# An LSTM scan whose wait for x's columns stands elsewhere, and a last attention written out by hand

## The chip, the cores and the metric

The kernel runs on one core of a Trainium2 chip. The metric is the device time of one execution in microseconds (us), the median over runs; lower is better. PE is TensorE, PEld its weight loads, DVE is VectorE, ACT is ScalarE, POOL is GpSimd and SP is SyncE, which here only issues DMAs.

## What is computed

Six layers run over 4 sequences of 512 tokens with 256 features: a gated recurrence, an LSTM with attention inside each step, a mixture of 8 experts, a second recurrence (here called the scan), a cross attention, and a mixture of 4 experts plus a shared one. Behind each stands a residual add and a layer norm without scale. Cut to the layers that the change touches:

```python
def step(carry, x_t):                       # the LSTM layer, 512 steps
    h, c, attn = carry
    gates = concat([x_t, attn]) @ W_ih.T + b_ih + h @ W_hh.T + b_hh
    i, f, g, o = split(gates, 4)
    c = sigmoid(f) * c + sigmoid(i) * tanh(g)
    h = sigmoid(o) * tanh(c)
    alpha = softmax((h @ Wq.T) @ context.T)  # over 512 source positions
    attn = tanh(concat([alpha @ context, h]) @ Wout.T + b_out)
...
x = layernorm(x + second_recurrence(x))
x = layernorm(x + softmax(q(x) @ k(ctx).T / 16) @ v(ctx))   # cross attention
x = layernorm(x + mixture(x))
```

## The kernel before, in words

Every engine has its own instruction list, and the lists meet at semaphores. A wait that is not yet met holds everything behind it on its engine.

**The LSTM.** Each step is one turn of a hardware loop (`Fori`) on PE, ACT, DVE, POOL and SP. The state has 256 hidden values in two halves, k = 0 and 1, so most names come in pairs: `c0`, `c1` for the cell, `h0`, `h1` for the hidden value. A turn of PE's loop (L938) begins with the attention scores: `part_scores(0, 0)` multiplies the first half of the hidden state with the keys (it waits for `h_ready[0]`), `part_scores(0, 1)` the second half (it waits for `h_ready[1]`). Then come softmax, the weighted sum, `select`, and `gates(t + 1)`. This last one starts with `o_gate_x_hid`, which adds x's share of the output gate. x's share of all gates was computed ahead of the scan and lies in DRAM (`xg_rows`). SP loads it step by step into the tile `lstm_xg` in two pieces: 12 KB for the three gates i, f, g and 4 KB for the output gate o. There is only one buffer, so SP issues the load of o's piece for the next step once PE has used the present one (`o_x_used`, in `gates`), and it signals `o_x_loaded`. Every wait of a loop compares a semaphore with a register, which the engine's sequencer computes from the turn's number.

On DVE a turn does: the transposes of the gates, `cell_products` and `new_cell` of half 0, the transpose of the output gate, `cell_products` of half 1, `new_hidden` of half 0, `new_cell` of half 1, `new_hidden` of half 1. `new_hidden` needs tanh of the cell from ACT, which needs `new_cell`.

**Behind the scan.** The second recurrence runs in slots (16 tiles of 32 steps and the output of the last tile). Beside it, as generators that give out work slot by slot, run the mixtures, the attention and their norms, in blocks (quarters) of 512 tokens. When the scan ends, the last matmuls of the third quarter's mixture and its norm are done, then the last quarter alone: the norm after the scan, the cross attention for the four batch entries, a norm, and the mixture of 28 chunks of weights. A norm (`StripNorm`) is a chain over three engines: mean (PE), deviation (DVE), squares (ACT), variance (PE), root (ACT), inverse (DVE), spread (PE), result (DVE).

## Time and profile before

| | |
|---|---|
| median of 3 runs | 5704.32 us (5700.22 to 5705.46) |
| the profiled execution: its own time | 5699.97 us |
| the profiled execution: its span | 5698.2 us |
| PE busy in the span | 91% |
| VectorE busy | 59% |
| ScalarE busy | 34% |
| the LSTM's scan, from about 191 us to 3903 us | 3712 us, 65% of the span |
| from 5460 us to the start of the last mixture's chunks at 5526.5 us | 66.5 us |

The span runs from the first to the last instruction of the trace; the execution's own time is 1.8 us longer. All times of rows below count from the span's start. PE's busy share alone doesn't tell a bound, since matmuls overlap each other; the idle time in front of a group, and who ended it, says more.

### The profile page before, as it was taken

To read this page: it belongs to the slowest core of one execution; us is meant where nothing else is said; L and a number is where in the kernel's file an instruction comes from. 1 tells how busy PE (TensorE), PEld (TensorE's weight loads), DVE (VectorE), ACT (ScalarE), POOL (GpSimd) and SP (SyncE) were. 2 spreads that over 40 slices of the span, in tenths; PEclk is the share of its full clock that TensorE was granted. 3 is DMA by queue.
4 is the path that set the end of the run, shared out by engine and by line. 5 is a ranking of instruction groups with operands and counts; after the bars stand their busy time and mean duration, and the time that the engine had idled before them with its cause. 6 is when DMAs were issued, how large, how long until landed. Compare 5 with 4: busy or idle time off the path is not lost. (4 is left out here: it accounts for less than half of the span.)

```text
span 5698.2 us, 474379 instructions
## 1 busy us (share of the span) xinstructions
PE 5170.7 (91%) x214184; PEld 4093.5 (72%) x214184; DVE 3385.5 (59%) x15403; ACT 1942.1 (34%) x7968; POOL 340.9 (6%) x795
## 2 busy tenths in 40 slices
PE   9899999999999999999999999998688879796989
PEld 4788888888888888888888888887434334443433
DVE  5455555555555555555555555554798999999941
ACT  2244444344444443444444434442212222222221
POOL 0000000000000000000000000000111111111100
PEclk9999999999999999999999999999899889897999
DMA  2000000000000000000000000002111101010111
GB/s 97 38 2 2 2 2 2 2 2 2 2 2 2 2 2 2 2 2 2 2 2 2 2 2 2 2 2 76 56 52 39 41 17 56 26 58 23 51 39 57
DMA packets 60806, 111.58 MB, mean 20 GB/s; under 512 B 18308, under 2 KB 28452, under 8 KB 60204
## 3 DMA queue, kind: packets, MB, share of 16 engines
q1 hardware_dynamic: 59276, 109.42, 6.3%
q10 hardware_dynamic: 1440, 1.06, 0.1%
q8 instruction: 46, 0.75, 0.1%
q14 instruction: 44, 0.36, 0.0%
HBM read 99.92 MB, written 10.52 MB: 19 GB/s over the span
## 5 line engine op out<-in xcount | busy, mean ns | idle before, releaser
L868 PE MATMUL lstm_part_ps<-lstm_keys,lstm_hid 128*8 128x64 f32 x65536 | 1041.8, 219 | 200.2 <-DVE lstm_hid L1039 200.2
L868 PEld LDWEIGHTS lstm_part_ps<-lstm_keys,lstm_hid 128*8 128x8 f32 x65536 | 920.1, 90 | 342.3 <-DVE lstm_hid L1039 313.5
L891 PE MATMUL lstm_ctx_ps<-lstm_values,lstm_alpha 128*8 128x128 f32 (+1 forms) x49152 | 1029.1, 237 | 0.0
L891 PEld LDWEIGHTS lstm_ctx_ps<-lstm_values,lstm_alpha 128*8 128x8 f32 x49152 | 919.1, 90 | 23.5
L1061 DVE TENSOR_REDUCE lstm_neg_max<-lstm_part_ps 128x1 f32<-128x64 f32 x1024 | 230.0, 225 | 729.0 <-PE lstm_part_ps L868 729.0
L1021 DVE STREAM_TRANSPOSE lstm_gates<-lstm_half_ps 128x96 f32<-128x96 f32 x1026 | 290.2, 283 | 588.6 <-PE lstm_half_ps L826 564.3
L826 PE MATMUL lstm_half_ps<-lstm_w_hid,lstm_hid 128*25 128x96 f32 x16384 | 578.9, 248 | 1.2 <-issue 1.2
L1000 ACT ACTIVATE lstm_expo<-lstm_part_ps,lstm_neg_max 128x64 f32<-128x64 f32 x1024 | 320.8, 313 | 621.1 <-DVE lstm_neg_max L1061 621.1
L826 PE MATMUL lstm_half_ps<-lstm_w_attn,lstm_attn 128*25 128x96 f32 x16448 | 437.0, 246 | 0.0
L989 ACT ACTIVATE lstm_cell<-lstm_gates 128x12 f32<-128x12 f32 x1024 | 225.3, 220 | 431.1 <-DVE lstm_gates L1021 431.1
L2115 ACT ACTIVATE mix_gated<-mix_gate_ps 128x512 f32<-128x512 f32 (+1 forms) x192 | 107.8, 561 | 743.3 <-PE mix_gate_ps L1842 738.4
L1852 PE MATMUL mix_up_ps<-mix_xw,mix_ring 128*128 128x512 f32 (+1 forms) x704 | 313.0, 580 | 41.0 <-DVE mix_weighted L2419 31.0
L826 PEld LDWEIGHTS lstm_half_ps<-lstm_w_attn,lstm_attn 128*25 128x25 f32 x16448 | 350.0, 104 | 0.2 <-issue 0.2
L1872 PE MATMUL mix_down_ps<-mix_weighted,mix_ring 128*128 128x512 f32 (+2 forms) x768 | 346.8, 575 | 0.8 <-DVE mix_weighted L2419 0.7
L1842 PE MATMUL mix_gate_ps<-xT,mix_ring 128*128 128x512 f32 (+2 forms) x768 | 346.6, 575 | 0.0
L826 PEld LDWEIGHTS lstm_half_ps<-lstm_w_hid,lstm_hid 128*25 128x25 f32 x16384 | 345.0, 104 | 1.4 <-issue 1.4
L1099 POOL TENSOR_TENSOR xT<-xT,lstm_attn 128x8 f32 x512 | 104.9, 205 | 3620.5 <-ACT lstm_attn L1014 3620.5
L826 PE MATMUL lstm_half_ps<-lstm_xg,lstm_masks 128*25 128x96 f32 x8224 | 311.9, 254 | 9.0 <-DVE lstm_attn L1047 9.0
L2392 DVE TENSOR_TENSOR rw_terms<-rw_state,rw_sc 128x384 f32<-128x384 f32 x512 | 296.7, 580 | 6.7
L997 ACT ACTIVATE lstm_tanh_c<-lstm_cell 128x4 f32<-128x4 f32 x1024 | 210.4, 205 | 194.6 <-DVE lstm_cell L1032 155.0
L1039 DVE SCALAR_TENSOR_TENSOR lstm_hid<-lstm_o_col,lstm_tanh_c 128x4 f32<-128x4 f32 x1024 | 171.1, 167 | 173.5 <-ACT lstm_tanh_c L997 139.2
L1872 PEld LDWEIGHTS mix_down_ps<-mix_weighted,mix_ring 128*128 128x128 f32 (+1 forms) x768 | 143.0, 193 | 182.3 <-issue 163.4
(333 smaller groups left out, 8485.7 us busy)
## 6 DMA issues: line engine op xcount, KB each, us to landing
mix_ring<-in_sm_chunks SPq DMA_DIRECT2D x112, 384.0 KB, 3.1
mix_ring<-in_mix_chunks SPq DMA_DIRECT2D x80, 384.0 KB, 3.1
lstm_xg<-xg_rows SPq DMA_DIRECT2D x514, 12.0 KB
lstm_xg<-xg_rows SPq DMA_DIRECT2D x513, 4.0 KB
xg_rows<-rec_lam SPq DMA_DIRECT2D x16, 512.0 KB, 2.6
xT<-in_xT SPq DMA_DIRECT2D x4, 512.0 KB, 9.3
ctxT<-in_ctxT SPq DMA_DIRECT2D x1, 2048.0 KB, 14.5
out_xT<-xT SPq DMA_DIRECT2D x4, 512.0 KB, 3.9
```

What stands on the lines that cost most here:

```text
L826: mm = pe.matmul(ps[j * STRIP:j * STRIP + ROWS, :], rows, w[:, j * HID + cols.start:j * HID + cols.stop], start=start, stop=stop)
L868: mm = pe.matmul(part_rows(score_ps[part], b), hid[:, k, lo:lo + SPACE], keys[:, k, b * SRC + c * SUB:b * SRC + (c + 1) * SUB], start=(n = ...
L891: mm = pe.matmul(part_rows(ctx_ps[n], b), alpha[:, b, c, SPACE - 1 - 2 * c:2 * SPACE - 1 - 2 * c], values[:, b * SC + c, ctx_cols[n]], sta ...
L989: act.activation(cell[:, k, 0:GATES - 1, :], by_batch(turned), ACT.Tanh).then_inc(half_tanh[k], 1)
L997: act.activation(tanh_c[:, k, :], cell[:, k, GATES - 1, :], ACT.Tanh, scale=0.5).then_inc(c_tanh[k], 1)
L1000: act.activation(expo[:, part, :], score_ps[part], ACT.Exp, bias=neg_max[:, part:part + 1]).then_inc(exp_ready, 1)
L1021: dve.transpose(gates[:, k, :], half_ps[k]).then_inc(half_turned[k], 1)
L1061: dve.tensor_reduce(neg_max[:, part:part + 1], score_ps[part], AX_X, ALU.max, negate=True)\
L1842: mm = pe.matmul(gate_ps[0:m, 0:width], ring[:, at, k * P:k * P + m], token_block(x, i)[:, k, :], start=(k == 0), stop=(k == KC - 1))
L1852: mm = pe.matmul(up_ps[lo:lo + piece, 0:width], ring[:, at, col:col + piece], xw[:, x.buffer(e), k, 0:width] if e < x.x.routed else token_ ...
L1872: mm = pe.matmul(down_ps[:, o_, 0:width], ring[0:m, gn % RING, lo + o_ * P:lo + (o_ + 1) * P], gw[0:m, gn % 2, 0:width], start=(n == 0), s ...
L2392: dve.tensor_tensor(terms[:, :, :, :], before.unsqueeze(1).to_broadcast([P, 3, HALF, HD]), sc[:, parity, UNIT_KEY:RECV + 1, t, :].unsqueez ...
```

## The change

Three edits. First, PE no longer waits for `o_x_loaded` inside `gates`: the wait stands at the top of the loop's turn, ahead of the scores, with the same threshold (the piece that `gates(t + 1)` of this turn will use). Second, on VectorE `new_cell` of half 1 comes ahead of `new_hidden` of half 0. Third, the last quarter's attention is a function of its own: its norm uses buffers and PSUM banks that the scan has left, it is interleaved with the third quarter's norm, and the four batch entries' scores have a bank each.

```diff
                 def o_gate_x_hid(t):
 
-                    pe.wait_ge(o_x_loaded, 16 * (t + 1))
                     gate_sums(o_gate_ps, o_cols, place, xg[:, :], start=True).then_inc(o_x_used, 1)
...
                 half_x(1).then_inc(half_x_used, 1)
+                pe.wait_ge(o_x_loaded, 16)
                 gates(0)
                 next_x(0)
                 with pe.Fori(0, SEQ) as t:
+                    pe.wait_ge(o_x_loaded, 16 * (t + 2))
                     pe.wait_ge(h_ready[0], t + 1)
                     part_scores(0, 0)
...
                     cell_products(t, 1)
+                    new_cell(t, 1)
                     new_hidden(t, 0)
-                    new_cell(t, 1)
                     new_hidden(t, 1)
...
+        last_prob = [gu[:, 0, :], gu[:, 1, :], last_sq[:, 0, :], last_sq[:, 1, :]]
+        last_prob_t = [gw[:, 0, :], gw[:, 1, :], last_d[:, 0, :], last_d[:, 1, :]]
...
+        last_ln = StripNorm(s, "last_ln", flat_b, flat_c, last_d, last_sq)
+        last_scores_ps = (gate_ps[:, :], up_ps[:, :], flat_b, flat_c)
+        last_turn_ps = (aux_ps, bank_a)
...
+                if x is SECOND and i == LAST_BLOCK - 1:
+                    yield from until_scanned("pe", LAST_BLOCK)
...
+                    pe.wait_ge(x_done, TILES)
+                    last_ln.mean(pe, lambda k: token_block(SECOND, LAST_BLOCK)[:, k, :], g.mean_mat[:, :], NB)
+                    down(count - 1)
+                    return
...
+            def last_attention():                       # PE
...
+                last_ln.variance(pe, 0, g.mean_mat[:, :], NB)
+                last_ln.spread(pe, 0, g.spread, NB)
+                pe.wait_ge(added, added_by_mixture(SECOND, before) + 1)
+                ln.mean(pe, lambda k: token_block(SECOND, before)[:, k, :], g.mean_mat[:, :], NB)
+                ln.variance(pe, n_before, g.mean_mat[:, :], NB)
+                ln.spread(pe, n_before, g.spread, NB)
+                pe.wait_ge(last_normed, 1)
...
+                for b in range(BATCH):
+                    scores(b)
+                turn(0)
+                turn(1)
+                output_of(0)
+                turn(2)
+                output_of(1)
+                turn(3)
+                output_of(2)
+                output_of(3)
...
+            def last_attention():                       # ACT
...
+                act.activation(warm[:, :], g.eps[:, :], ACT.Exp)
...
+                exponential(0)
+                exponential(1)
+                exponential(2)
+                keep_turned(0)
+                exponential(3)
+                for b in range(1, BATCH):
+                    keep_turned(b)
+                act.activation(warm[:, :], g.eps[:, :], ACT.Sqrt)
...
+            def last_attention():                       # DVE
...
+                last_ln.inverse(dve, 0, NB)
+                ln.deviation(dve, n_before, before, NB)
+                last_ln.result(dve, 0, block_x, NB).then_inc(last_normed, 1)
+                ln.inverse(dve, n_before, NB)
+                ln.result(dve, n_before, before, NB).then_inc(ln_done, 1)
+                maximum(0)
+                maximum(1)
+                maximum(2)
+                probabilities(0)
+                maximum(3)
+                for b in range(1, BATCH):
+                    probabilities(b)
```

The scaling by 1/16 of the maxima and the product with the inverse sums, on ACT before, are on DVE in the last quarter. The rest of the last quarter (the mixture) is as it was.

In PE's list at the top of the LSTM's loop there stood, before:

```order
L938 UNCONDITIONAL_BRANCH
L938 ISA
L868 MATMUL lstm_part_ps<-lstm_keys,lstm_hid 8x64 [waits lstm_h0_ready]
L868 MATMUL lstm_part_ps<-lstm_keys,lstm_hid 8x64 x15
L868 MATMUL lstm_part_ps<-lstm_keys,lstm_hid 8x64 [waits lstm_h1_ready]
```

and now stands:

```order
L938 ISA
L940 REGISTER_ALU [waits lstm_o_x_loaded]
L867 MATMUL lstm_part_ps<-lstm_keys,lstm_hid 8x64 [waits lstm_h0_ready]
L867 MATMUL lstm_part_ps<-lstm_keys,lstm_hid 8x64 x15
L867 MATMUL lstm_part_ps<-lstm_keys,lstm_hid 8x64 [waits lstm_h1_ready]
```

The first scores of a step have a register instruction ahead of them that holds the wait for x's columns; it computes the number with which the next wait compares.

Further down in the same turn of PE's loop, from the last `select` to x's share of the output gate (`lstm_ctx_ps<-lstm_xg`), there stood:

```order
L909 MATMUL lstm_attn_ps<-lstm_sel_scaled,lstm_out_row 32x4 [waits lstm_out_row1_ready]
L909 MATMUL lstm_attn_ps<-lstm_sel_scaled,lstm_out_row 32x4 x3
L849 ISA
L826 MATMUL lstm_ctx_ps<-lstm_xg,lstm_masks 25x64 [waits lstm_o_x_loaded]
L826 MATMUL lstm_ctx_ps<-lstm_xg,lstm_masks 25x64 x3
L826 MATMUL lstm_ctx_ps<-lstm_w_hid,lstm_hid 25x64 x8
```

and now stands:

```order
L908 MATMUL lstm_attn_ps<-lstm_sel_scaled,lstm_out_row 32x4 [waits lstm_out_row1_ready]
L908 MATMUL lstm_attn_ps<-lstm_sel_scaled,lstm_out_row 32x4 x3
L826 MATMUL lstm_ctx_ps<-lstm_xg,lstm_masks 25x64 x4
L826 MATMUL lstm_ctx_ps<-lstm_w_hid,lstm_hid 25x64 x8
```

The register computation (`ISA`) and the wait between the two groups are gone.

Behind the scan, DVE's list had, from the add of the scan's last output on:

```order
L2445 TENSOR_TENSOR xT<-mix_down_ps,xT 128x2x512
L98 TENSOR_TENSOR mix_weighted<-xT,mix_gate_ps 128x1024
L2371 TENSOR_TENSOR xT<-xT,rw_bank_a 128x2x4x32
L121 RECIPROCAL tail_ln_rstd<-tail_ln_rstd 128x128
L132 TENSOR_TENSOR xT<-mix_weighted,mix_gate_ps 128x2x512
```

and has now:

```order
L2489 TENSOR_TENSOR xT<-xT,rw_bank_a 128x2x4x32
L98 TENSOR_TENSOR last_d<-xT,rw_bank_b 128x1024
L2566 TENSOR_TENSOR xT<-mix_down_ps,xT 128x2x512
L121 RECIPROCAL last_ln_rstd<-last_ln_rstd 128x128
L98 TENSOR_TENSOR mix_weighted<-xT,mix_gate_ps 128x1024
L132 TENSOR_TENSOR xT<-last_d,rw_bank_b 128x2x512
```

The last quarter's deviation (`last_d`) has moved ahead of the third quarter's add (`xT<-mix_down_ps`), and the third quarter's own norm (`tail_ln`, `mix_weighted`) behind it.

## Rows read from the trace of the kernel before

**Rows 1.** The profile's page, first line.

```profile
span 5698.2 us, 474379 instructions
```

**Rows 2.** Busy time by stage: stretch, its length, busy of each engine, PEclk, DMA share.

```profile
191.00:3903.00 3712.00, 3509.61 (x208488) 3249.95 (x208488) 1897.80 (x11753) 1487.96 (x7154) 104.72 (x511) 1.00 0.01 2
5460.00:5482.28 22.28, 12.42 (x66) 7.39 (x66) 8.70 (x9) 3.22 (x5) 3.51 (x5) 0.74 0.38 130
5489.52:5511.00 21.48, 17.36 (x96) 11.94 (x96) 3.32 (x8) 9.80 (x21) 0.00 (x0) 1.00 0.00 1
```

**Rows 3.** Timeline of one LSTM step: start, length, instruction, idle before and its end.

```profile
2001.62 1.85 PEld L868 LDWEIGHTS lstm_part_ps<-lstm_keys,lstm_hid 128*8 128x8 f32 x128 [0.61 <-DVE lstm_hid L1039]
...
2006.52 0.15 PEld L826 LDWEIGHTS lstm_ctx_ps<-lstm_xg,lstm_masks 128*25 128x25 f32 x8
...
2008.66 0.17 DVE L1039 SCALAR_TENSOR_TENSOR lstm_hid<-lstm_o_col,lstm_tanh_c 128x4 f32<-128x4 f32 x1
2008.74 0.16 DVE L1032 SCALAR_TENSOR_TENSOR lstm_cell<-lstm_uv 128x4 f32<-128x4 f32 x1
2008.88 1.85 PEld L868 LDWEIGHTS lstm_part_ps<-lstm_keys,lstm_hid 128*8 128x8 f32 x128 [0.61 <-DVE lstm_hid L1039]
...
2009.17 0.17 DVE L1039 SCALAR_TENSOR_TENSOR lstm_hid<-lstm_o_col,lstm_tanh_c 128x4 f32<-128x4 f32 x1 [0.27 <-ACT lstm_tanh_c L997]
```

**Rows 4.** Groups of instructions, 200 to 3900 us: count, busy, idle before, releaser.

```profile
L868 PEld LDWEIGHTS lstm_part_ps<-lstm_keys,lstm_hid 128*8 128x8 f32 x65280 | 916.5, 90 | 341.1 <-DVE lstm_hid L1039 312.3
```

**Rows 5.** Timeline of SP's queue, 2006.8 to 2008: the 4 KB load.

```profile
2007.06 0.64 SPq L802 DMA_DIRECT2D lstm_xg<-xg_rows  x1
```

**Rows 6.** Windows of 0.1 us behind that issue; last columns PEclk, DMA share, GB/s.

```profile
2008.50:2008.60 0.10, 0.00 (x0) 0.00 (x0) 0.10 (x2) 0.10 (x1) 0.00 (x0) 1.00 0.15 33
2008.60:2008.70 0.10, 0.00 (x0) 0.00 (x0) 0.04 (x1) 0.03 (x1) 0.00 (x0) 1.00 0.01 0
```

**Rows 7.** Timelines and a window at the first step: the 12 KB load.

```profile
187.87 0.62 SPq L802 DMA_DIRECT2D lstm_xg<-xg_rows  x1
...
189.50:189.60 0.10, 0.10 (x12) 0.10 (x8) 0.00 (x0) 0.10 (x1) 0.00 (x0) 0.50 0.11 31
...
190.14 0.40 PEld L826 LDWEIGHTS lstm_half_ps<-lstm_xg,lstm_masks 128*25 128x25 f32 x16 [0.24 <-DMA lstm_xg<-xg_rows]
```

**Rows 8.** Line 849's instructions, and PE's timeline around them.

```profile
L849 PEldq FUSED_REGOPS  x512: 37/37/37, 198.9 to 3908.2; - x171
...
2006.22 0.22 PE L909 MATMUL lstm_part_ps<-lstm_sel_scaled,lstm_out_row 128*32 128x4 f32 x8
2006.28 0.34 PE L826 MATMUL lstm_half_ps<-lstm_w_hid,lstm_hid 128*25 128x96 f32 x8
2006.44 0.22 PE L909 MATMUL lstm_attn_ps<-lstm_sel_scaled,lstm_out_row 128*32 128x4 f32 x8
2006.53 0.29 PE L826 MATMUL lstm_ctx_ps<-lstm_xg,lstm_masks 128*25 128x64 f32 x5
```

**Rows 9.** Chain that ended last, in order of time, 5440 to 5530 us.

```profile
5461.34 3.78 PE mix_gate_ps L93 x4
...
5472.42 1.97 PE mix_gate_ps L93 x4
5474.41 1.23 DVE mix_weighted L98
5475.67 1.06 ACT mix_gated L102
...
5478.89 2.09 PE mix_gate_ps L127 x8
...
5482.28 3.78 PE mix_gate_ps L1976 x4
...
5489.52 2.00 PE mix_gate_ps L1945 x4
...
5511.00 1.42 DVE xT L2491 x2
...
5516.82 1.28 ACT L116
```

More of the change, by code:

```diff
@@ L1415 @@
 KV_AFTER = 2
+LAST_BLOCK = len(LAST_BLOCKS) - 1
 def norm_after_mixture(x, i):
-    return i if x is FIRST else NORMS + 3 * i + 2
+    return i if x is FIRST else NORMS + 3 * i + 2 - (i == LAST_BLOCK)
 def norm_after_scan(q):
@@ L1426, in norm_after_attention @@
 def norm_after_attention(q):
-    return NORMS + 3 * q + 1
+    return NORMS + 3 * q + 1 - (q == LAST_BLOCK)
 def added_by_mixture(x, i):
@@ L1702, in side_by_side, with background @@
                 pass
-        def background(engine, mixture, keys_values, attention):
+        def background(engine, mixture, keys_values, attention, last_attention):
             for i in range(1, len(FIRST_BLOCKS)):
@@ L1710, in background @@
                         yield from keys_values(b, KV_SLOTS)
-            for q in range(len(LAST_BLOCKS)):
+            for q in range(LAST_BLOCK):
                 yield from until_scanned(engine, q)
@@ L1714, in background @@
                 yield from mixture(SECOND, q, SLOTS)
+            last_attention()
+            yield from mixture(SECOND, LAST_BLOCK, SLOTS)
         @block.sync
@@ L2007, in attention, with scores, turn, output_of @@
                 yield from pause(slots)
+            def last_attention():
+                q, before = LAST_BLOCK, LAST_BLOCK - 1
+                own = NB // BATCH
+                n_before = norm_after_mixture(SECOND, before)
+                def scores(b):
+                    for k in range(KC):
+                        mm = pe.matmul(last_scores_ps[b], queries[:, k, b * own:(b + 1) * own], keys[:, k, b * SRC:(b + 1) * SRC],
+                                       start=(k == 0), stop=(k == KC - 1))
+                    mm.then_inc(scores_ready, 1)
+                def turn(b):
+                    pe.wait_ge(prob_ready, BATCH * q + b + 1)
+                    if b >= 2:
+                        pe.wait_ge(turn_kept, BATCH * q + b - 1)
+                    for kc in range(SC):
+                        mm = pe.transpose(last_turn_ps[b % 2][:, kc * P:(kc + 1) * P], last_prob[b][:, kc * P:(kc + 1) * P], ident[:, :])
+                    mm.then_inc(turned, 1)
+                def output_of(b):
+                    pe.wait_ge(turn_kept, BATCH * q + b + 1)
+                    for o_ in range(KC):
+                        for kc in range(SC):
+                            mm = pe.matmul(down_ps[:, o_, b * own:(b + 1) * own], values[:, b * SC + kc, o_ * P:(o_ + 1) * P],
+                                           last_prob_t[b][:, kc * P:(kc + 1) * P], start=(kc == 0), stop=(kc == SC - 1))
+                    mm.then_inc(attended, 1)
+                last_ln.variance(pe, 0, g.mean_mat[:, :], NB)
[5 more added lines that the diff above has]
+                pe.wait_ge(last_normed, 1)
+                for o_, ps in enumerate((flat_b, flat_c)):
+                    for k in range(KC):
+                        mm = pe.matmul(ps, ca_w["q"][:, k, o_ * P:(o_ + 1) * P], token_block(SECOND, q)[:, k, :],
+                                       start=(k == 0), stop=(k == KC - 1))
+                    mm.then_inc(query_ready, 1)
+                pe.wait_ge(query_kept, KC * (q + 1))
+                pe.wait_ge(ln_done, n_before + 1)
+                for b in range(BATCH):
[8 more added lines that the diff above has]
+                output_of(3)
+                pe.wait_ge(added, added_by_attention(q) + 1)
+                ln.mean(pe, lambda k: token_block(SECOND, q)[:, k, :], g.mean_mat[:, :], NB)
+                ln.variance(pe, norm_after_attention(q), g.mean_mat[:, :], NB)
+                ln.spread(pe, norm_after_attention(q), g.spread, NB)
@@ L2017, in _ @@
             project_gate(0)
-            side_by_side("pe", scan_slot, background("pe", mixture, keys_values, attention))
+            side_by_side("pe", scan_slot, background("pe", mixture, keys_values, attention, last_attention))
         @block.scalar
@@ L2129, in mixture @@
                     yield from pause(chunk_slots(n, slots, x.width(i)))
+                if x is SECOND and i == LAST_BLOCK - 1:
+                    yield from until_scanned("act", LAST_BLOCK)
+                    return
                 yield from pause(slots)
@@ L2208, in _ @@
             project_gate(0, 0)
-            side_by_side("act", scan_slot, background("act", mixture, keys_values, attention))
+            side_by_side("act", scan_slot, background("act", mixture, keys_values, attention, last_attention))
         @block.gpsimd
@@ L2443, in mixture @@
                     yield from pause(chunk_slots(n, slots, x.width(i)))
+                if x is SECOND and i == LAST_BLOCK - 1:
+                    yield from until_scanned("dve", LAST_BLOCK)
+                    last_ln.deviation(dve, 0, token_block(SECOND, LAST_BLOCK), NB)
                 dve.wait_ge(down_ready, x.at(i, x.count))
                 dve.tensor_tensor(block_x, down_ps[:, :, 0:width], block_x, ALU.add).then_inc(added, 1)
+                if x is SECOND and i == LAST_BLOCK - 1:
+                    return
                 yield from pause(slots)
@@ L2530, in _ @@
                 project(t, 0, 0)
-            side_by_side("dve", scan_slot, background("dve", mixture, keys_values, attention))
+            side_by_side("dve", scan_slot, background("dve", mixture, keys_values, attention, last_attention))
 class Shared:
```

52 lines of the change are left out of this document (added).

## The prediction

> **What bounds the kernel now.** I read the page first, then the busy time by stage, because an edit inside a loop of 512 turns and an edit behind it are worth very different amounts. The span is 5698.2 us [rows 1], and 3712 us of it are the LSTM's scan [rows 2]. So 0.02 us per step are 10 us, while the stretch from 5460 us to the end of the last attention is some 51 us in all.
>
> Next, one step in the timeline [rows 3]. The scores of successive steps start at 2001.62 and 2008.88, so a step takes 7.26 us. PE is the engine that matters: through the whole step the scores are the one place where its weight loads stand still for long, 0.61 us, and `lstm_hid` ends that wait. Over 510 steps the weight loads of the scores idle 341.1 us, of which 312.3 us are the start (0.61 a step); the other 28.8 us, 0.056 us a step, lie inside the group [rows 4]. That is the second half: `new_hidden` of half 1 runs from 2009.17 to 2009.34, and the first 32 products, at 128 in 1.85 us less this small wait, would be done some 0.45 us after 2008.88. The chain through a step is thus hidden state, scores, softmax, weighted sum, select, attention, gates, cell, hidden state. All engines hand over within it; a delay at the top of PE's loop is a delay of the step unless a later wait swallows it.
>
> **The moved wait.** The time that decides is when the 4 KB of the output gate land. PE uses the old piece at 2006.52 [rows 3]; SP issues the next load at 2007.06, 0.54 us later [rows 5]; the scores, behind the new wait, start at 2008.88, which is 1.82 us after the issue. Before the change nobody needed this load until the next `gates`, more than 4 us later, so its lateness was hidden. Now it stands ahead of 128 weight loads and everything that hangs on them.
>
> When does it land? The trace has no wait for this load, so I bound it. From below: data still moves in the slice that ends at 2008.60, and a trace of it in the next [rows 6], so the load is not there before 1.55 us. From above: the 12 KB load at the start of the scan is issued at 187.87 and PE, idle for 0.24 us on the DMA, goes on at 190.14 [rows 7], 2.27 us later. There the last slice with traffic ends at 189.60, so 0.54 us pass between the last data and the released engine. The same 0.54 us behind 2008.60 gives 2009.14, or 2.08 us after the issue. The packets are smaller here, so I take a little less, 2.02 us; it is nearer to the row with the same queue, tile and waiting engine than to the bare end of the data.
>
> The Trainium skill (DMA: Bandwidth & Descriptors, Anatomy of one DMA) says that a DMA has a fixed cost of about 2.0 us, and that the semaphore moves only when the last byte is confirmed. An estimate by that page, 2.0 us plus 0.01 us for 4 KB, would put the landing 0.19 us behind the present start of the scores; it speaks against this change, and rows 7 agree that the release comes well after the data.
>
> On top comes the form of the wait: it hangs on a register instruction, and the first product compares with the number that this instruction computes. The instruction itself is like the 0.037 us one of line 849 [rows 8]. The products behind that one start about 0.09 us after the pair before; without it about 0.06 us (next step). I take 0.08 us from the release to the first weight load, between 0.04 and 0.10.
>
> So scores can start at 2007.06 + 2.02 + 0.08 = 2009.16, 0.28 us later than now. Part of it is paid already: the wait of 0.056 us for half 1 vanishes, since the hidden state is then long there. Cost: 0.28 - 0.056 = 0.22 us a step.
>
> **What the removed wait gives back.** Between the last select and the output gate's products stood the register computation. The same 8 select instructions are followed after 0.06 us by the next group where nothing stands between (2006.22 to 2006.28), and after 0.09 us here (2006.44 to 2006.53) [rows 8]. Gain 0.03 us, from 0 (if the attention's tanh, which is due next, takes the place) to 0.03. PE works without a pause from there into the attention's products, so I take all of it.
>
> **The second cell first.** `new_cell` of half 1 starts 0.08 us after `new_hidden` of half 0 [rows 3]. Swapped, h1 comes about 0.1 us earlier and h0 about 0.05 us later. Alone that trades 0.056 us of waiting for half 1 against 0.05 us at the start: nothing to 0.02 us. Under the new wait both are early, and the edit is worth 0. Its cover is the DMA; without that it is worth up to 10 us over the scan, and at the worst it costs 10 us.
>
> **The scan's sum.** 0.22 - 0.03 = 0.19 us a step, times 511 steps with a preceding turn, is 97 us, call it 98.
>
> **Behind the scan.** Costs first. PE now leaves the last down product and the third quarter's mean for after the scan's output, so it stands idle until then, and its clock is at half: four such products took 3.78 us at the lower clock and 1.97 us at the upper [rows 9]; the granted clock was 0.74 of full in this stretch already [rows 2]. The scan's output comes perhaps 0.7 us sooner, near 5467.8. From a norm's mean to the queries took 9.86 us (5472.42 to 5482.28) [rows 9]. In the new order the queries also stand behind the third quarter's mean (1.97 to 3.78), deviation (1.23), squares (1.06), variance, root and inverse (about 2 together) and spread (up to 2.09), less the result's 1.23 that is hidden: they start at about 5485 to 5489 where they started at 5482.28, 3 to 7 us later. The mean, squares and spread had hidden under the scan's last output before; this cover is gone.
>
> Gains: the attention from first scores to last output takes 21.48 us now, in which PE is busy 17.36 us [rows 2], because each pair of banks waits for the exponentials. With four banks the scores follow each other (4 x 1.72 us), and one turn and output after another follows: I get about 18 us, 3.3 us less. The table load of 1.28 us ahead of the root [rows 9] moves under other work and gives about 0.6 us. If the queries' eight products run at the full clock, another 2.5 us return. Net: +3 to +7, -3.9, and 0 to -2.5 us: between -3 and +3. I take 0. The output's DMA and the weight loads behind it on SP's queue start some 14 us later, but the weights are wanted only at 5526, so that is hidden.
>
> **Sum.** 5700.0 (the execution's own time) + 98 + 0 = 5798 us. That execution stood 4 us under the median of the runs shown; I put the prediction at 5799.
>
> **Rivals.** A change of less than 0.2% (11 us) can't be told from none here.
>
> *The load has landed in time (faster).* If the release comes within 1.82 us of the issue, less the 0.08 us of the register, PE never waits. Then 0.03 us are won at the gates and up to 0.02 us by the swap: 0.03 to 0.04 us x 511 = 15 to 20 us, 5680 to 5685. For it: the data is through at 1.55 us. Against it: in rows 7 the release took 0.54 us more. 9 in 100.
>
> *A little late.* A release 1.74 to 1.85 us after the issue costs what the 0.056 us and the gain at the gates cover, to 0.03 us more: 5690 to 5720. 6 in 100.
>
> *The clock.* PE's idle stretch ahead of the scores grows from 0.61 to 0.9 us. If that let the granted clock fall from 1.00 [rows 2] to 0.5 in the scan, the products would take twice as long, at least 1.5 us a step, and the time would pass 6400. The stretches that did fall to the lower level had PE idle for over 2 us. The Trainium skill (TensorE: Matmul & The Clock Gate, Part 1) says that activity releases the gate and idleness closes it; by it such an end would be possible, and nothing in the scan's rows shows it. 2 in 100.
>
> *Later than thought.* If the 4 KB need the full 2.27 us, the cost is 0.53 - 0.056 - 0.03 = 0.44 us a step: 5925. 5 in 100.
>
> **How the numbers follow.** The main case has 78 in 100. Its spread comes from the release with its register: each 0.02 us is 10 us. From 2.00 us to 2.19 us in all it gives 5700 + 48 to 5700 + 145, so 5745 to 5845; with the tail's 3 us and a share of the late case I give 5740 to 5845. Faster by over 0.2%: 9 in 100; within 0.2%: 4; slower: 87.
>
> **What would show it.** After the change the PE weight loads of the scores should idle about 0.9 us a step with the DMA of `lstm_xg` as what ended it, a step should take 7.45 us, `lstm_hid` of both halves should be written before the scores start, and the output gate's products should follow the select after 0.06 us. Behind the scan the queries should start later relative to its last add, and the four scores should follow without a pause. The prediction fails if the scores still wait for `lstm_hid`: then the load lands sooner than I think. It fails in size if the register costs more than 0.1 us or the swap is not covered.

## The result and the profile after

| | before | changed |
|---|---|---|
| median | 5702.55 us (5700.22 to 5705.46, 4 runs) | 5772.00 us (5766.06 to 5776.21, 4 runs) |
| ratio | | 1.0121, 95% interval 1.0103 to 1.0138 |
| profiled execution, own time | 5699.97 us | 5770.81 us |
| first to last write of `lstm_hid` (the scan) | 3712.8 us | 3790.6 us |

The change costs 69.5 us at the median and 70.8 us between the two profiled executions. The forecast was 5799 us with a range of 5740 to 5845: slower, as forecast, and the loss three quarters of the 95 us that it named. The scan alone grew by 77.8 us; what is behind it gave 6 to 7 us back.

The page of the changed kernel, its first line and two groups of part 5 (line, engine, operation, count, busy us, mean ns, idle before and its releaser):

```profile
span 5769.0 us, 474380 instructions
...
L867 PE MATMUL lstm_part_ps<-lstm_keys,lstm_hid 128*8 128x64 f32 x65536 | 1010.4, 219 | 327.3 <-DMA lstm_xg<-xg_rows 326.9
L867 PEld LDWEIGHTS lstm_part_ps<-lstm_keys,lstm_hid 128*8 128x8 f32 x65536 | 920.0, 90 | 438.0 <-DVE lstm_hid L1040 438.0
```

The weight loads of the scores now stand idle for 438.0 us instead of 341.1 [rows 4], 0.86 us a step instead of 0.67. The matmuls' line names the load of `lstm_xg` as the releaser, a name that no wait of the scan carried before. The weight loads' line still names `lstm_hid`, since the semaphore on that instruction itself is `h_ready[0]`; the wait for x's columns hangs on the register instruction ahead of it. Here the two lines have to be read together.

One step of the changed kernel in the timeline (start, length, instruction, idle before):

```profile
2001.64 1.80 PEld L867 LDWEIGHTS lstm_part_ps<-lstm_keys,lstm_hid 128*8 128x8 f32 x128 [0.81 <-DVE lstm_hid L1040]
...
2006.37 0.16 PEld L908 LDWEIGHTS lstm_attn_ps<-lstm_sel_scaled,lstm_out_row 128*32 128x32 f32 x8
...
2006.43 0.15 PEld L826 LDWEIGHTS lstm_ctx_ps<-lstm_xg,lstm_masks 128*25 128x25 f32 x8
...
2008.64 0.17 DVE L1040 SCALAR_TENSOR_TENSOR lstm_hid<-lstm_o_col,lstm_tanh_c 128x4 f32<-128x4 f32 x1
...
2008.99 0.17 DVE L1040 SCALAR_TENSOR_TENSOR lstm_hid<-lstm_o_col,lstm_tanh_c 128x4 f32<-128x4 f32 x1 [0.19 <-ACT lstm_tanh_c L998]
2009.02 1.80 PEld L867 LDWEIGHTS lstm_part_ps<-lstm_keys,lstm_hid 128*8 128x8 f32 x128 [0.83 <-DVE lstm_hid L1040]
...
2009.03 1.97 PE L867 MATMUL lstm_part_ps<-lstm_keys,lstm_hid 128*8 128x64 f32 x128 [0.61 <-DMA lstm_xg<-xg_rows]
```

and in the same step SP's queue:

```profile
2006.97 0.64 SPq L802 DMA_DIRECT2D lstm_xg<-xg_rows  x1
```

A step takes 2009.02 - 2001.64 = 7.38 us here and 7.41 us as a mean over 500 steps, against 7.26 before. The first hidden half is written at 2008.81, and yet the scores start at 2009.02, 0.21 us later; before, 0.05 us lay between the two [rows 3]. The second half, written from 2008.99 to 2009.16, is not there yet when the scores start, but they need it only behind their first quarter. The scores start 2.05 us after the issue of the load.

Behind the scan, the chain that ended last (start, length, engine, tile, line):

```profile
5533.17 0.32 ACT rw_var L2157
...
5541.74 3.45 PE rw_bank_b L93 x4
5545.21 1.23 DVE last_d L98
...
5550.85 1.73 PE mix_gate_ps L93 x4
5552.61 1.23 DVE mix_weighted L98
...
5557.53 2.07 PE mix_gate_ps L127 x8
5559.61 2.87 PE rw_bank_b L2070 x4
...
5564.97 1.98 PE mix_gate_ps L2041 x4
5566.95 1.72 PE mix_up_ps L2041 x4
5568.67 1.72 PE rw_bank_b L2041 x4
5570.38 1.73 PE rw_bank_c L2041 x4
...
5582.38 1.42 DVE xT L2659 x2
...
5593.82 3.57 PE mix_aux_ps L1254 x4
```

The third quarter's norm (`mix_gate_ps`, `mix_weighted`) stands in this chain ahead of the queries (line 2070). The four scores follow each other without a pause, and the attention lasts from 5564.97 to 5582.38, 17.41 us instead of 21.48 [rows 2].

### The profile page after: what moved, and what is told of

Same layout as the page of the kernel before. It is cut to its first block and busy times, and to the rows that moved or that the text cites. A ratio compares the mean times of both kernels' runs of the same rounds, so it can differ in the third digit from the quotient of the medians.

```text
span 5769.0 us, 474380 instructions
## 1 busy us (share of the span) xinstructions
PE 5108.1 (89%) x214184; PEld 4054.2 (70%) x214184; DVE 3396.0 (59%) x15411; ACT 1939.1 (34%) x7962; POOL 341.7 (6%) x795
## 5 line engine op out<-in xcount | busy, mean ns | idle before, releaser
L867 PE MATMUL lstm_part_ps<-lstm_keys,lstm_hid 128*8 128x64 f32 x65536 | 1010.4, 219 | 327.3 <-DMA lstm_xg<-xg_rows 326.9
L867 PEld LDWEIGHTS lstm_part_ps<-lstm_keys,lstm_hid 128*8 128x8 f32 x65536 | 920.0, 90 | 438.0 <-DVE lstm_hid L1040 438.0
L826 PEld LDWEIGHTS lstm_half_ps<-lstm_w_attn,lstm_attn 128*25 128x25 f32 x16448 | 321.6, 103 | 8.7 <-issue 0.2
L1869 PEld LDWEIGHTS mix_up_ps<-mix_xw,mix_ring 128*128 128x128 f32 x704 | 127.8, 190 | 198.5 <-issue 135.4
```

The source lines that it names most:

```text
L826: mm = pe.matmul(ps[j * STRIP:j * STRIP + ROWS, :], rows, w[:, j * HID + cols.start:j * HID + cols.stop], start=start, stop=stop)
L867: mm = pe.matmul(part_rows(score_ps[part], b), hid[:, k, lo:lo + SPACE], keys[:, k, b * SRC + c * SUB:b * SRC + (c + 1) * SUB], start=(n = ...
L1869: mm = pe.matmul(up_ps[lo:lo + piece, 0:width], ring[:, at, col:col + piece], xw[:, x.buffer(e), k, 0:width] if e < x.x.routed else token_ ...
```

## The experiments

The kernels ran in three series, each beside the kernel before on the same chip (5702.52, 5701.56 and 5698.36 us): the first four of the table, then the three whose wait or product stands elsewhere in the changed kernel and the last row, then the rest. The scan's length is that from the first to the last write of `lstm_hid` in the profiled execution.

| kernel | median us | ratio to before (95%) | scan us | against before |
|---|---|---|---|---|
| moved wait alone | 5785.77 | 1.0143 (1.0127 to 1.0158) | 3797.8 | +85.0 |
| swap alone | 5696.64 | 0.9987 (0.9978 to 0.9996) | 3706.4 | -6.4 |
| last attention alone | 5703.09 | 0.9997 (0.9988 to 1.0006) | 3716.6 | +3.8 |
| changed, wait in the gates | 5693.29 | 0.9984 (0.9975 to 0.9993) | 3707.1 | -5.7 |
| changed, wait behind the scores | 5674.08 | 0.9952 (0.9939 to 0.9966) | 3691.2 | -21.6 |
| changed, wait between the halves | 5671.73 | 0.9948 (0.9935 to 0.9962) | 3691.3 | -21.5 |
| x's share multiplied early | 5749.88 | 1.0085 (1.0071 to 1.0098) | 3759.3 | +46.5 |
| two buffers, loops of two steps | 7670.75 | 1.3450 (1.3432 to 1.3468) | 5708.1 | +1995.3 |
| before, wait behind the scores | 5686.86 | 0.9975 (0.9965 to 0.9986) | 3699.8 | -13.0 |
| changed, load of 1 KB | 5676.60 | 0.9958 (0.9944 to 0.9971) | 3688.5 | -24.3 |
| changed, once more | 5761.75 | 1.0105 (1.0089 to 1.0120) | 3775.1 | +62.3 |
| wait behind, norm under the queries | 5665.20 | 0.9938 (0.9924 to 0.9951) | 3689.1 | -23.7 |

### The three edits, one by one

**The wait alone.** The kernel before with

```diff
-                    pe.wait_ge(o_x_loaded, 16 * (t + 1))
                     gate_sums(o_gate_ps, o_cols, place, xg[:, :], start=True).then_inc(o_x_used, 1)
...
                 with pe.Fori(0, SEQ) as t:
+                    pe.wait_ge(o_x_loaded, 16 * (t + 2))
                     pe.wait_ge(h_ready[0], t + 1)
```

> The kernel before with only the wait for x's columns moved to the top of the loop's turn. Theory A (the wait alone makes the loss: the 4 KB land after the hidden state is ready): the scan grows by 70 to 85 us, as it did from before to after (some 78 us), and as the part behind the scan is that of before, the total is 5775 to 5788. The weight loads of the scores idle about 0.85 us a step and no wait for the second half is left. Rival B (the loss needs the swapped cell update too, because the first hidden half comes later there): clearly less, under 5760.

Measured: 5785.77 us, and the scan 85.0 us longer. Its chief waits from 191 to 3975 us (who waited for whom, us in total, times, longest):

```profile
PEld lstm_part_ps L867 <- DVE lstm_hid L1040: 443.5, 509, 1.0
...
PE lstm_part_ps L867 <- DMA lstm_xg<-xg_rows: 333.5, 509, 0.8
```

The weight loads' wait is 0.87 us a step, against 0.86 in the changed kernel. The total lies in theory A's range, and the whole loss is this edit's; rival B falls.

**The swap alone.** The kernel before with

```diff
                     cell_products(t, 1)
+                    new_cell(t, 1)
                     new_hidden(t, 0)
-                    new_cell(t, 1)
                     new_hidden(t, 1)
```

> The kernel before with only the cell update of half 1 ahead of the new hidden state of half 0. Theory A: the first half comes about 0.04 us later and the wait for the second half (0.056 us a step) is gone, so 0.016 us a step are won: 8 us, total 5690 to 5700. Rival B (the swap delays the start of the scores by more than it saves): above 5705, up to 5720 at a loss of 0.03 us a step.

Measured: 5696.64 us; the scan is 6.4 us shorter, 0.013 us a step. A small gain, by the interval at least 0.04%. The weight loads start 0.05 us behind the first hidden half as before, and the second half no longer makes them wait: all 338.1 us of the wait for `lstm_hid` come from the start of the scores.

**The last attention alone.**

> The kernel before with only the last attention written out (both other edits undone). Theory A (the last attention wins some 3 us from the last hidden output to the mixture's first chunk, as the chain of before and after shows: queries 3.8 us later, attention 4.1 us shorter, the keeping of the queries 1.9 and the root 0.6 us shorter): 5696 to 5703. Rival B (the 3.7 us more that were won between the two scans' ends in the changed kernel belong to this edit as well): 5694 to 5697, and the second recurrence is shorter up to its last output. Rival C (nothing): 5702 to 5706.

Its edit is the third one of the diff ahead of the prediction. Measured: 5703.09 us, no change that can be told; it lies in the range of rival C (nothing), at the upper edge of theory A's. The scan, in which nothing was edited, is 3.8 us longer in this profile. From the last scan output's variance (`rw_var`) to the mixture's router logits (`mix_router_logit_rows` on ACT), the stretch that the edit rewrites, the traces show 65.8 us here against 67.0 before.

**The two small edits together.** The changed kernel, with its wait back in the gates:

> The changed kernel with the wait for x's columns back inside the gates; the swap and the last attention stay. Theory A: the sum of the two other edits, 8 and 3 us under before: 5685 to 5698. Rival B (the edits hang together, for example the second hidden half is late again): 5700 or more.

Measured: 5693.29 us, 9 us under before and 3 us under the swap alone. The two edits by themselves gave 5 us together (5.9 less and 0.6 more); the 4 us between the sum and this kernel are within what the intervals leave open, and nothing shows that the edits hinder each other.

### Where the wait may stand

**Behind all scores.**

```diff
                 with pe.Fori(0, SEQ) as t:
-                    pe.wait_ge(o_x_loaded, 16 * (t + 2))
                     pe.wait_ge(h_ready[0], t + 1)
...
                     part_scores(1, 1).then_inc(scores_ready, 1)
+                    pe.wait_ge(o_x_loaded, 16 * (t + 2))
                     pe.wait_ge(exp_ready, 2 * t + 1)
```

> The changed kernel with the wait for x's columns not ahead of the scores but right behind all four score groups (before the first turn of the exponentials). Theory A (the place of the wait alone makes the loss; the load has landed by then): the loss is gone, total at most that of the kernel with the wait inside the gates (5693 us); if the 0.03 us a step that the gates win by the missing register computation stays won, 5674 to 5684. Rival B (the register computation and wait cost as much in the new place, since PE has no idle time there): 5690 to 5697. Rival C (the position at the top is not what costs): above 5750.

Measured: 5674.08 us. The loss of 70 us turns into a gain of 27. Against the kernel with the wait in the gates (of another series) it is 19 us, of which the scan shows 15.9 us or 0.031 us a step: the removed register computation's price, won because the wait now stands where it is met.

**Between the first and the second half** (the same line behind `part_scores(0, 0)`).

> The changed kernel with the wait between the scores' products of the first and of the second half of the hidden state, 0.40 us behind the start of the scores. Theory A (the load lands on average some 0.1 us, and at the latest some 0.3 us, behind the natural start of the scores): nothing is lost, the total is that of the kernel with the wait behind all scores, within 8 us. Rival B (the load lands later than the records of its completion say, for instance because PE sees it late): 0.1 us a step or more lost, 50 us above that kernel.

Measured: 5671.73 us, and the scan is the same to 0.1 us. So a wait 0.4 us behind the start of the scores costs nothing. This bounds the load's lateness from above without a record of the load itself; by the completion records of this trace it lands 0.05 us behind the start of the scores on average and 0.20 at the latest. Taken with the wait at the top, it shows how steep the edge is: 0.4 us further up in PE's list costs 90 to 100 us (the changed kernel ran in other series).

**The same move without the other edits** (the kernel before, the wait behind all scores).

> The kernel before with only the wait taken from the gates and put behind all four score groups; old cell order, old last attention. Theory A (the missing register computation ahead of the output gate's products is worth 0.03 us a step by itself): 5682 to 5692. Rival B (the gain of 20 us that the kernel with all three edits showed over the one with the wait in the gates needs the swap too): 5695 or more.

Measured: 5686.86 us, in the range of theory A, and a scan 13.0 us shorter: 0.025 us a step by itself.

### What makes the load late

**x's share multiplied early.** The wait stays at the top; the products that free the buffer stand ahead of the first select:

```diff
                     pe.wait_ge(out_row_ready[0], t + 1)
+                    o_gate_x()
                     select(0)
...
                 def gates(t):
 
-                    o_gate_x_hid(t)
+                    o_gate_hid()
```

> The changed kernel, wait at the top of the turn, but x's share of the output gate is multiplied earlier, ahead of the first select instead of behind the last, so that its buffer is free and the next 4 KB are requested some 0.34 us earlier in the step. Theory A (the loss is the lateness of the load, 1.96 us from issue to landing on average): the load lands before the hidden state is written in most steps, and the step falls from 7.41 to 7.21 to 7.28 us; total 5675 to 5710. Rival B (a wait at the top of the turn costs by its form, also when it is met): the step stays at 7.35 or more, total above 5745.

Measured: 5749.88 us. Theory A's number fails, and rival B's (a step of 7.35 us or more, over 5745 us) is met; the timeline shows that its reason is not:

```profile
2001.67 1.79 PEld L870 LDWEIGHTS lstm_part_ps<-lstm_keys,lstm_hid 128*8 128x8 f32 x128 [0.66 <-DVE lstm_hid L1045]
...
2006.12 0.21 PEld L826 LDWEIGHTS lstm_ctx_ps<-lstm_xg,lstm_masks 128*25 128x25 f32 x8
...
2006.26 0.19 PEld L911 LDWEIGHTS lstm_part_ps<-lstm_sel_scaled,lstm_out_row 128*32 128x32 f32 x8
...
2006.72 0.18 ACT L1020 ACTIVATE lstm_attn<-lstm_part_ps 128x4 f32<-128x4 f32 x1 [0.61 <-PE lstm_part_ps L911]
...
2008.80 0.17 DVE L1045 SCALAR_TENSOR_TENSOR lstm_hid<-lstm_o_col,lstm_tanh_c 128x4 f32<-128x4 f32 x1
...
2009.02 1.79 PEld L870 LDWEIGHTS lstm_part_ps<-lstm_keys,lstm_hid 128*8 128x8 f32 x128 [0.66 <-DVE lstm_hid L1045]
```

The scores start at 2009.02, 0.05 us behind the hidden half that ends at 2008.97: the wait at the top is met and costs nothing (over 500 steps the load lands 0.31 us before the first half is written, and the scores start 0.05 us behind it), so rival B's reason is refuted. And yet a step takes 7.35 us. The eight early weight loads push the first select from 2006.12 to 2006.26, and the attention's tanh goes with it: it starts 0.60 us after 2006.12, where in the kernel with the wait behind the scores 0.46 us pass from the first weight load of the select to the tanh. That is 0.14 us, and the steps differ by 0.13. Over 500 steps the first select starts 4.59 us behind the scores here and 4.45 there; the rest of the step is the same in both within 0.01 us. I had held the products ahead of the select for covered by those that the gates still have to do; they were not, since the tanh waits for the select itself.

**Two buffers.** The load is requested a whole step earlier. The loops of TensorE and SyncE are written out for two steps, since each buffer needs its own instructions:

```diff
-                with pe.Fori(0, SEQ) as t:
-                    pe.wait_ge(o_x_loaded, 16 * (t + 2))
+                with pe.Fori(0, SEQ // 2) as u:
+                  for n in range(2):
+                    t = 2 * u + n
+                    pe.wait_ge(o_x_loaded[1 - n], 16 * (u + 1 + n))
...
-                    gates(t + 1)
+                    gates(t + 1, 1 - n)
```

> The changed kernel, wait at the top of the turn, but with two buffers for the output gate's x columns (the loops of TensorE and SyncE are written out for two steps), so that each 4 KB are requested a whole step earlier. Theory A (the loss at the top is the lateness of the load and nothing else): the wait is met on arrival, the scores start 0.05 us behind the hidden state as before the change, and the total is that of the kernels whose wait stands behind the start of the scores, 5665 to 5690. Rival B (a wait at the top costs by its register instruction or form even when it is met): 5700 or more, up to 0.08 us a step or 41 us above those kernels.

Measured: 7670.75 us, far outside of both. The page of this kernel, queues and a group of part 5:

```profile
q8 instruction: 1192, 19.53, 1.1%
...
L872 PEld LDWEIGHTS lstm_part_ps<-lstm_keys,lstm_hid 128*8 128x8 f32 x65536 | 1160.7, 101 | 1185.6 <-issue 1096.2
```

the same queue on the page of the changed kernel:

```profile
q8 instruction: 46, 0.75, 0.1%
```

and the two-buffer kernel's timeline at the end of a turn:

```profile
2017.54 0.17 DVE L1047 SCALAR_TENSOR_TENSOR lstm_hid<-lstm_o_col,lstm_tanh_c 128x4 f32<-128x4 f32 x1 [0.18 <-ACT lstm_tanh_c L1005]
2021.83 0.55 PEld L872 LDWEIGHTS lstm_part_ps<-lstm_keys,lstm_hid 128*8 128x8 f32 x24 [5.08 <-issue]
```

Both hidden halves are there by 2017.71, and PE's next weight load starts 4.1 us later, put down to issue, that is to nothing that it waited for. Meanwhile the queue that carries instructions moved 19.53 MB instead of 0.75: 18.78 MB over 256 turns is 73 KB a turn. Two transfers of 16 KB on this queue start within the stop, at 2017.43 and 2017.67, and take 2.0 and 1.5 us. My reading is that the loop of two steps no longer stays with the engine and is fetched anew in every turn; no run varied the length of the loop's body alone, so this cause is read from the page, not shown by itself. The Trainium skill (Runtime: NRT & Kernel Launch, Instruction fetch mechanics) says that a taken branch whose target is outside of the pages that the engine holds forces a fetch of the target before it can go on; the queue's row agrees. The question that the run was made for stays unanswered by it.

**A load of 1 KB.** The changed kernel, the load cut to the first of its four quarters; x's share of the other three quarters of the output gate is left out of the computation (their products still run, over columns that hold zero, so PE's work is the same).

```diff
-                    sp.dma_start(quarters(xg[0:BATCH, :])[:, :, part],
-                                 quarters(xg_dram[bass.ds(t * BATCH, BATCH), :])[:, :, part]).then_inc(loaded, 16)
+                    n = 1 if part is o_part else QUARTERS
+                    sp.dma_start(quarters(xg[0:BATCH, :])[:, 0:n, part],
+                                 quarters(xg_dram[bass.ds(t * BATCH, BATCH), :])[:, 0:n, part]).then_inc(loaded, 16)
```

> The changed kernel, but each load of the output gate's x columns brings only the first of four quarters, 1 KB in place of 4 KB (the other three quarters of x's share of the output gate are left out of the computation). Theory A (the time from issue to landing is a fixed cost, not one of bytes): the total is that of the changed kernel within 15 us, 5757 to 5787. Rival B (the bytes or the number of packets carry the latency): a tenth of a microsecond or more per step less, under 5730.

Measured: 5676.60 us, 85 us under the changed kernel of the same series. My theory A falls: the time from issue to landing is no fixed cost. SP's queue in this kernel:

```profile
2008.23 0.26 SPq L803 DMA_DIRECT2D lstm_xg<-xg_rows  x1
```

and windows of 0.1 us behind this issue (last columns PEclk, DMA share, GB/s):

```profile
2009.10:2009.20 0.10, 0.10 (x10) 0.10 (x8) 0.10 (x2) 0.09 (x2) 0.00 (x0) 1.00 0.06 10
2009.20:2009.30 0.10, 0.10 (x9) 0.01 (x2) 0.10 (x2) 0.10 (x2) 0.00 (x0) 1.00 0.00 0
```

The instruction itself takes 0.26 us instead of 0.64, and the data pass 0.87 to 0.97 us after the issue, where those of the 4 KB pass 1.4 to 1.6 us after it (the changed kernel's issue is at 2006.97):

```profile
2008.37:2008.47 0.10, 0.05 (x4) 0.00 (x0) 0.10 (x2) 0.10 (x1) 0.00 (x0) 1.00 0.12 28
2008.47:2008.57 0.10, 0.00 (x0) 0.00 (x0) 0.07 (x3) 0.09 (x1) 0.00 (x0) 1.00 0.07 13
2008.57:2008.67 0.10, 0.00 (x0) 0.00 (x0) 0.10 (x2) 0.00 (x0) 0.00 (x0) 1.00 0.00 0
```

By the completion records of the traces, over 500 steps, the load lands 1.28 us after its issue instead of 1.93 (the changed kernel once more, same series). Most of the gain of 0.65 us lies ahead of the data and not in their flow: the first packet starts 0.89 us after the issue instead of 1.43 (means over 500 steps), which is 0.54 us; from the first packet's start to the last one's end it takes 0.10 us instead of 0.17, and from there to the landing 0.30 instead of 0.33. The 4 KB are 4 rows of 4 pieces of 256 bytes, the 1 KB 4 rows of one piece; with 12 pieces fewer the instruction is 0.38 us shorter. It fits a cost per piece. Bytes and pieces were changed together, and 4 KB in four pieces of 1 KB were not tried (it needs another layout of `xg_rows`), so which of the two carries the cost is open. With this load in time, the kernel with the wait at the top is as fast as those whose wait stands later (scan 3688.5 us against 3691.2): the lateness is the whole loss.

**The changed kernel once more.**

> The changed kernel once more. The kernel with the moved wait alone took 14 us more than it, while the edits between them (swap and last attention) should give some 3 to 9 under the moved wait. Theory A (the swap is hidden and the rest is a difference of 0.016 us in the mean time from issue to landing between the two profiles, which does not belong to the kernel): here a time between 5772 and 5784 and a landing 1.96 to 1.98 us after the issue. Rival B (that difference belongs to the kernel): 5766 to 5776 again, landing at 1.96 us.

Measured: 5761.75 us (5758.25 to 5764.52), outside of both numbers. Its load lands 1.934 us after the issue on average, where the first profile of the same program had 1.960 and the kernel with the wait alone 1.976. With the program unchanged the latency moved by 0.026 us and the scan by 15.5 us (3790.6 and 3775.1), 0.030 us a step. The kernel before lies at 1.984, the four kernels of the first series at 1.976 to 1.985, those of the later ones at 1.93 to 1.94. The 0.016 us that theory A wanted to explain are less than this, so they need not belong to the kernel, as it claimed; its number failed. Kernels whose wait is covered feel less of it: the kernel before moved by 4 us over the three series.

### A version that beats both

The wait behind all scores, and behind the scan most of the third quarter's norm taken off the path to the queries. ScalarE's and VectorE's lists follow the new order, and the first two scores use the banks of the queries. On PE:

```diff
                 last_ln.variance(pe, 0, g.mean_mat[:, :], NB)
-                last_ln.spread(pe, 0, g.spread, NB)
                 pe.wait_ge(added, added_by_mixture(SECOND, before) + 1)
                 ln.mean(pe, lambda k: token_block(SECOND, before)[:, k, :], g.mean_mat[:, :], NB)
-                ln.variance(pe, n_before, g.mean_mat[:, :], NB)
-                ln.spread(pe, n_before, g.spread, NB)
+                last_ln.spread(pe, 0, g.spread, NB)
                 pe.wait_ge(last_normed, 1)
...
+                ln.variance(pe, n_before, g.mean_mat[:, :], NB)
                 pe.wait_ge(query_kept, KC * (q + 1))
+                scores(0)
+                ln.spread(pe, n_before, g.spread, NB)
+                scores(1)
                 pe.wait_ge(ln_done, n_before + 1)
-                for b in range(BATCH):
-                    scores(b)
+                scores(2)
+                scores(3)
```

> The kernel with the wait behind all scores, and behind the scan the third quarter's norm taken off the path to the queries: its mean stands ahead of the last norm's spread, its variance behind the queries, its spread between the first two scores, and the first two scores use the banks of the queries. Theory A (in the changed kernel the queries and scores wait for the third quarter's norm): the last score ends some 7 us sooner, 5 to 8 us less than the kernel with the wait behind all scores. Rival B (the clock falls in the new idle places or the third quarter's result is late for the third score): between 3 us less and 3 us more.

Measured: 5665.20 us, 9 us under the kernel with the wait behind the scores (5 to 8 were forecast), 36 us (0.6%) under before and 97 to 107 us under the changed kernel, which ran in other series. Its chain behind the scan:

```profile
5449.49 3.78 PE mix_gate_ps L93 x4
...
5454.43 1.23 DVE xT L132
5455.70 1.98 PE rw_bank_b L2068 x4
5457.69 1.73 PE rw_bank_c L2068 x4
5459.44 0.69 ACT ca_queries L2301
5460.18 1.98 PE rw_bank_b L2041 x4
5462.16 0.89 PE mix_gate_ps L127 x8
5463.05 1.72 PE rw_bank_c L2041 x4
```

The queries follow right behind the last norm's result (`xT` L132); of the third quarter's norm its mean (`mix_gate_ps` L93), 3.78 us ahead of that result, and its spread (`mix_gate_ps` L127) are left in the chain. Counted from `rw_var`, the last score ends 6.1 us sooner than in the kernel with the wait behind the scores. From `rw_var` to the router logits it takes 61.8 us, against 67.5 in that kernel and 67.0 before. The two profiles differ by 14.4 us in all, 6.6 of them in stretches up to `rw_var` where nothing was edited, so a part of the 9 us between the medians may lie there too.

## Why the prediction was right, step by step

**What bounds the kernel.** Right: a delay at the top of PE's loop was a delay of the step. The runs add what I had not said: with the wait there, the loop's cycle runs through other stations. It goes scores, output gate's products, SP's issue, landing, scores; cell and hidden state lie beside it, and the first half is written 0.25 us before the scores start, on average. This is why the swap is worth nothing under the moved wait.

**The term "scores 0.28 us later".** Measured over 500 steps: PE's use to SP's issue 0.543 us (forecast 0.54), issue to landing 1.960 (2.02), landing to the first weight load 0.117 (0.08), in all 2.62 us where 2.36 passed before. So 0.26 instead of 0.28. The landing came 0.06 us sooner and the hand-over through the register instruction took 0.04 us more than taken; that the two errors nearly cancel is luck. The choice to put the landing near rows 7 instead of at the bare end of the data was the one that decided the sign: the data passed 1.6 us after the issue, and 1.6 would have forecast a gain.

**The vanishing wait for the second half, 0.056 us.** Right in size: 0.059 us less from the scores to the last select. The reason given was too strong, that both halves would long be written and the second before the scores start: it is written 0.11 us after their start on average, and before it in only 7 of 100 steps. The wait vanishes because the first quarter of the scores takes 0.45 us.

**The removed wait, 0.03 us.** Too small here: from the weight loads of the last select to those of x's share it takes 0.057 us instead of 0.106, so 0.049 us. In the kernel before, where the attention's tanh runs beside it, the same edit gave 0.025 us a step. Under the moved wait the path to SP's issue alone counts, and no tanh covers a part.

**The scan's sum.** Forecast 0.28 - 0.056 - 0.03 = 0.19; measured 0.26 - 0.059 - 0.049 = 0.152 us, times 511 is 78 us against 98 forecast. These are the terms that were mis-sized: 0.02 us in the landing with its hand-over and 0.02 in the gates. The size of the loss also belongs to the series: the same program, once more, lost 63 us.

**The swap.** Forecast alone nothing to 0.02 us a step, under the wait 0. Alone it gave 0.013 us. The total of the kernel that has it with the wait at the top is 14 us lower than that of the wait alone, but not by the swap: in the two traces the path from the scores to the use of x's columns (4.79 us), from there to SP's issue (0.54) and from the landing to the scores (0.12) agree to 0.001 us, and the latency alone differs, by 0.016 us a step or 8 us. The rest lies behind the scan. The two kernels were not run in one series.

**Behind the scan.** Forecast between -3 and +3. Counted from `rw_var` (5459.61 us before, 5533.17 after), the queries start 3.8 us later (forecast 3 to 7), their own stretch to the scores is 1.9 us shorter by the clock (0 to 2.5), the attention takes 17.4 us (18) and the root wins 0.6 us (0.6): 2.7 us less in all. In the second profile of the same program this stretch took 68.1 us instead of 64.3, in others with the same code 64.3 to 67.5. The stretches at half clock (granted clock 0.50) fell elsewhere: in the 68 us behind `rw_var` they add up to 27.3 us in the first profile of this program and to 36.4 in the second. The nine profiles with the new attention have a mean of 65.9 us, the four with the old one 67.0; so the edit's worth is 1 us on average, and nothing can be told from a single profile. The other 3.6 us behind the scan fell between the scan's end and `rw_var`, ahead of the edited stretch. The same stretch took 1549.6 to 1562.0 us in the thirteen profiles of kernels with one-step loops.

**The rivals.** "The load has landed in time" was the right price for the kernels in which it is so: 5680 to 5685 forecast, 5671.73 and 5674.08 measured, with the last attention's few us below. "The clock" did not happen: with PE's stop ahead of the scores at 0.86 us, the granted clock from 191 to 3980 us is 1.00. (That stretches at the lower level had PE idle for over 2 us is not so for all of them: before, the granted clock fell to 0.50 at 5682.4 us, and PE had stood still for 1.32 us from 5680.67.)

```profile
191.00:3980.00 3789.00, 3459.53 (x208454) 3216.39 (x208440) 1903.45 (x11749) 1487.43 (x7152) 104.27 (x511) 1.00 0.01 2
```

The rule of the Trainium skill that I weighed (DMA: Bandwidth & Descriptors, Anatomy of one DMA), some 2.0 us fixed, was near the 1.96 us of the 4 KB. The page states that fit for a DMA issued from GpSimd, and the load of 1 KB landed after 1.28 us. As a constant for a load issued by SP the runs refute it; that it was near was luck of this size.

## What to carry to other kernels

Before a wait is moved up, find when its event comes, not only that nobody has waited for it so far: a load that was 0.16 us too late for its new place went unseen in a trace without any wait on it. A cheap check is the same wait a few instructions further down: here 0.4 us in PE's list parted 60 to 70 us of loss from 30 of gain. And where a program sits on a DMA's latency, look at its pieces as well as its bytes (which of the two carries the cost is open here), and expect its time to vary from one series of runs to the next by more than a kernel's whose waits are covered.

## What the runs showed that I had not expected

- A load of 4 rows by 4 pieces of 256 bytes keeps SP's queue for 0.64 us and lands 1.93 to 1.98 us after its issue; 4 rows by one piece take 0.26 us and land after 1.28.
- The mean latency of the same load differed by 0.026 us between two profiles of the same program, and by up to 0.05 us between kernels of different series.
- A hardware loop written out for two steps on TensorE and SyncE took 3.9 us a step more than the loop of one step (scan 5708.1 against 3712.8 us over 512 steps), with 73 KB of instructions moved per turn.
- An edit behind the scan moved the scan by 3.8 us (0.007 us a step, the last attention alone), and the stretch from the scan's end to `rw_var` varied by 12 us between profiles of kernels that hardly differ there. Differences of that size in one profile say nothing about an edit.
